# Products of constants on TensorE in four waits between the MLP and the shared units

## The reference

```python
x = x + ln(attention(ln(x), sign-quantised weights))        # 32 heads, 8 key heads, causal
x = x + ln(W2 @ fwht(silu(W1 x) * (W3 x)))                  # MLP, hidden 1024, layer 0
k, v, r = mixes of ln(x) with the row before it, @ Wk, Wv, Wr
x = x + ln((scan over time of k, v) * r @ Wo)               # layer 1, first part
out = sum over the 4 best of 32 experts of c * (silu(x @ wg) * (x @ wu)) @ wd
out = out + sigmoid(x @ seg) * (silu(x @ sg) * (x @ su)) @ sd   # shared expert, 704 wide
x = x + ln(out)
```

## Time and profile before

| | us |
|---|---|
| median of 3 runs | 558.63 |
| lowest and highest | 557.62, 561.06 |
| the profiled execution | 553.65 |
| its span, first to last instruction | 551.8 |
| PE busy | 429.5 (78% of the span) |
| DVE, ACT, POOL busy | 351.8, 271.5, 226.7 |
| mean granted TensorE clock | 0.903 of full |

### The profile page before, as it was taken

The page is one execution under the profiler, slowest core; times in us unless marked ns, Lnnn a source line. Parts: engine busy times, 40 slices in busy tenths (PEclk is TensorE's granted clock), DMA queues, the critical chain, the costliest instruction groups (busy, mean ns, idle before and its releaser), DMA issues.

```text
span 551.8 us, 9885 instructions
## 1 busy us (share of the span) xinstructions
PE 429.5 (78%) x3364; PEld 296.1 (54%) x3364; DVE 351.8 (64%) x857; ACT 271.5 (49%) x519; POOL 226.7 (41%) x301
## 2 busy tenths in 40 slices
PE   2887979998996889696994170687879799999754
PEld 1635435554552378585873160466768466666443
DVE  5558848788871447737468889597663355555336
ACT  8457646766777342233861462332452255556402
POOL 5881424434649402501500452138448045565600
PEclk9979979999999779899999585788989899999958
DMA  7583531111410259100000000699712244454282
GB/s 219 142 135 116 89 58 45 34 40 45 170 37 4 76 172 330 49 1 1 0 2 0 29 29 29 169 210 273 223 51 100 78 123 143 128 143 121 64 310 77
DMA packets 52033, 56.04 MB, mean 102 GB/s; under 512 B 10244, under 2 KB 42893, under 8 KB 51984
## 3 DMA queue, kind: packets, MB, share of 16 engines
q1 hardware_dynamic: 47536, 46.67, 32.0%
q0 software_dynamic: 4448, 8.73, 4.7%
HBM read 35.61 MB, written 21.73 MB: 104 GB/s over the span
## 4 chain that ended last, share of the span: by engine, by line
PE 51%; DVE 22%; issue 7%; ACT 6%; DMA 6%; SPq 4%; POOL 4%; DVEq 0%; ACTq 0%; POOLq 0%
PE ps L2249 7%; PE ps L1982 5%; PE ps L2032 4%; PE ps L1961 4%; PE ps L1940 4%; PE ps L2272 4%; PE ps L2020 4%; PE ps L2230 3%; PE ps L2022 3%; PE ps L2021 3%; DVE st L937 2%; PE ps L1994 2%; DVE h_lo L1104 2%; ACT probs L1625 2%; DMA q_ring<-q_ring 2%
## 5 line engine op out<-in xcount | busy, mean ns | idle before, releaser
L1625 ACT ACTIVATE probs<-ps 128x512 f32<-128x512 f32 x160 | 87.2, 598 | 44.8 <-PE ps L1961 44.0
L1037 DVE TENSOR_REDUCE negm<-ps 128x2 f32<-128x1024 f32 (+1 forms) x64 | 67.6, 1082 | 17.1 <-PE ps L1950 17.0
L845 POOL DMA_INDIRECT y_slots_scratch<-yblk,ids x48 | 47.0, 979 | 49.9 <-issue 29.0
L679 POOL TENSOR_TENSOR rstd<-ve,halfneg 128x4 f32<-128x4 f32 x15 | 16.2, 1078 | 110.3 <-DVE ve L966 46.9
L1982 PE MATMUL ps<-probs,v_all 128*32 128x128 f32 (+3 forms) x512 | 50.6, 475 | 4.9 <-DVE att L1065 3.5
L1940 PE MATMUL ps<-k_all,q_ring 64*128 64x512 f32 (+3 forms) x256 | 46.6, 375 | 8.4 <-DMA q_ring<-q_ring 6.5
L1663 ACT CAST h_hi<-hf 128x512 fp32r<-128x512 f32 x28 | 17.4, 621 | 65.8 <-DVE hf L1095 63.7
L1961 PE MATMUL ps<-q_ring,k_all 64*128 64x512 f32 (+3 forms) x256 | 40.8, 375 | 9.0 <-ACT probs L1625 6.8
L1436 DVE COPY xcol<-ps 128x256 f32<-128x256 f32 x48 | 20.4, 425 | 39.3 <-PE ps L2230 39.3
L1961 PEld LDWEIGHTS ps<-q_ring,k_all 64*128 64x128 f32 x256 | 21.1, 188 | 42.0 <-ACT probs L1625 31.7
L814 POOL DMA_INDIRECT x_sorted_scratch<-rows,dest x32 | 33.0, 1032 | 24.5 <-DVE dest L1353 15.6
(11 more groups left out here) (329 smaller groups left out, 1326.9 us busy)
## 6 DMA issues: line engine op xcount, KB each, us to landing
x_sorted_scratch<-pad SPq DMA_DIRECT2D x6, 1072.0 KB, 12.7
xblk<-x_sorted_scratch SPq DMA_DIRECT2D x96, 67.0 KB
wgu<-in_moe_w SPq DMA_DIRECT2D x4, 1536.0 KB, 17.6
q_ring<-q_parts_scratch SPq DMA_DIRECT2D x64, 64.0 KB
ycomb<-y_slots_scratch SPq DMA_DIRECT2D x8, 512.0 KB, 6.4
wd<-in_moe_w SPq DMA_DIRECT2D x1, 3072.0 KB, 18.8
sraw<-in_moe_w SPq DMA_DIRECT2D x6, 384.0 KB, 3.0
q_parts_scratch<-qparts SPq DMA_DIRECT2D x4, 512.0 KB, 4.9
```

Of the source, the lines that this page charges most:

```text
L845: pool.indirect_dma_start(out=y_slots, out_offset=bass.IndirectOffsetOnAxis(ap=ids[:, i:i + 1], axis=0), in_=yblk[:, i % YR, :], in_offset ...
L1037: dve.tensor_reduce(negm[:, par, :, hp, qt], pair_of, AX.X, ALU.max, negate=True).then_inc(s1_read, 1)
L1625: act.activation(probs[:, par, u, :], ps[:, col_unit(g, u), :], ACT.Exp)\
```

## The change

Four calls of `keep_busy` are added to PE's stream, all with bank 0: 44 products ahead of `transposes(2, 1)`, 20 between them and `keys(1)`, 60 between `values(1)` and `transposes(3, 0)`, 14 between `receptances(1)` and `logits_of(0)`. Each call stands ahead of the wait that follows it.

```diff
             mlp_down(B * HC - 1)
+            keep_busy(44, 0)
             pe.wait_ge(rows_ready, 4 * TPB)
             transposes(2, 1, rows_tile(1))
+            keep_busy(20, 0)
             keys(1)
             mix_out(0)
             values(1)
+            keep_busy(60, 0)
             pe.wait_ge(rows_ready, 5 * TPB)
             transposes(3, 0, rows_tile(0))
             receptances(1)
+            keep_busy(14, 0)
             logits_of(0)
             logit_rows(0)
             shared_up(0)
```

## The result

The changed kernel takes 555.6 us (median of 20 runs), the kernel before 557.84 (20 runs). The ratio is 0.9937, 95% interval [0.9913, 0.9962]: 3.5 us less, between 2.1 and 4.9. It leaves out the slower of two groups into which executions fall, and is not the quotient of the two medians, which lie 2.2 us apart. Forecast were 556.0 us and a gain of 2.6.

A forecast was written before the change was run, and what follows sets the result against it. Short PE bursts alternate with DVE, ACT and POOL row work, slowed by a clock that falls in idle waits. Gains 0.6 + 1.13 + 1.84 = 3.57 us, less 1.0 for one fall, take 2.6 off 558.63: 556.0 us, range 551.5 to 560.0.

The forecast's parts named there:

- Lengths of the fillings: The four PE fillings last 9.8, 4.6, 13.4 and 3.2 us at full clock, each ending within its wait.
- Transposes of turn 2: Eight transposes before the keys run at full clock, 1.09 us instead of 1.97; ACT's copies limit the gain to 0.6 us.
- Keys: Key products at full clock finish before DVE asks, removing its waits of 0.48 and 0.65 us; gain 1.13 us.
- Transposes of turn 3 and receptances: From the transposes to the seventh product, 4.31 us becomes 2.47 at full clock; all counts, gain 1.84 us.
- Routing products gain nothing: Routing products behind the fourth filling already run at full clock, 0.40 us each, so they gain nothing.
- What follows keeps it: Mask, destinations, scatters and first load of sorted rows descend from the logits, so the load comes about 2.6 us sooner.
- The fall of the clock: One fall of PE's clock, in the idleness before turn 2's transposes or in `mix_out`, takes 1.0 us off the gain.
- rival 2: The clock holds throughout the stretch, the full 3.57 us is gained, 555.1 us; chance 0.13.
- Rival 3: Transposes don't speed up in this place, gain only 1.1 us, 557.5 us; chance 0.03.
- Rival 4: Over 1% faster, some 552.6 us, if the runs lose more at half clock here than the trace; chance 0.12.
- Rival 5: Gain swallowed by a later burst falling to half clock, or fillings not holding the clock; 558.6 us, chance 0.14.
- Rival 6: Slower: the two short fillings run wholly at half clock, late by 3.2 and 2.2 us; 564.0 us, chance 0.08.

The follow-up runs named there:

- Experiment 5: The changed kernel with 100 products in place of 60 in the third filling; ratio 1.0052 to the kernel before, 562.37 us.
- experiment 2: The changed kernel without the 44 and the 60, so only the 20 and the 14 stay; ratio 1.0009 to the kernel before.
- experiment 3: The changed kernel with each filling halved to 22, 10, 30 and 7 products; ratio 1.0006 to the kernel before.
- experiment 7: The changed kernel with ten more products inside `mix_out(0)`; ratio 0.99 to the kernel before.
- experiment 8: The changed kernel with fillings lengthened to 52, 24, 67 and 17 and ten more products inside `mix_out(0)`; ratio 0.9916 to the kernel before.
- experiment 10: The changed kernel with only the first site filled (44 and 20), the 60 and 14 removed; ratio 0.9995 to the kernel before.
- experiment 12: The changed kernel with 10 products in `mix_out(0)` and 10 more in the wait for DVE's mask; ratio 0.9861 to the kernel before.
- experiment 4: The changed kernel with each filling product replaced by one f32 transpose of the 128x128 identity, same counts; ratio 0.9999 to the kernel before.
- experiment 11: The kernel before, same code, profiled again for a second trace; 558.75 us against 553.65 for the first profiled execution.
- experiment 1: The changed kernel without the 20 and the 14, so only the 44 and the 60 stay; ratio 0.9983 to the kernel before.
- experiment 9: The changed kernel with only the second site filled (60 and 14), the 44 and 20 removed; ratio 0.9989 to the kernel before.

## Why the prediction was right, step by step

- **Lengths of the fillings**: predicted 9.8, 4.6, 13.4, 3.2; measured 9.67, 4.48, 13.12, 3.20. Right (0.216 us a product, where I took 0.22), and that no filling was late in the changed kernel decided the sign. Experiment 5 shows the price of being late.
- **Transposes of turn 2**: 0.6 predicted, 0.76 measured (keys at 18.84 for 19.60). ACT's two copies now run one behind the other.
- **Keys**: 1.13 predicted, 0.74 measured. DVE's two waits are gone, and `cols_lo` begins 1.32 us sooner behind the keys' start, but it grew by 0.58. In the trace of before it ran behind POOL's work on the shared chunk; now it meets it. DVE and POOL, before:

```profile
323.67 0.68 DVE L1161 TENSOR_TENSOR cols_lo<-den,cols_hi 128x512 fp32r<-128x512 f32 x1
```

```profile
321.24 1.84 POOL L806 TENSOR_TENSOR schunks<-sraw,schunks 128x768 fp32r<-128x768 f32 x1
```

and in the second trace of the changed kernel:

```profile
324.70 1.26 DVE L1161 TENSOR_TENSOR cols_lo<-den,cols_hi 128x512 fp32r<-128x512 f32 x1
```

```profile
323.61 1.81 POOL L806 TENSOR_TENSOR schunks<-sraw,schunks 128x768 fp32r<-128x768 f32 x1
```

  `cols_lo` lasts 1.26 us instead of 0.68, and ends 0.54 us behind POOL's step (325.42). In all nine traces in which it begins during that step (the first and second of the changed kernel, experiments 2, 3, 5, 7, 8, 10 and 12) it takes 1.26 or 1.27; in the five others it begins after it and takes 0.68. The waits that I counted as the gain were time in which POOL had been getting out of the way. The Trainium skill, "VectorE: DVE Perf Modes", section "Two Vector instructions with no wait between them", speaks of a second SBUF read interface that VectorE shares with GpSimd, used by an instruction with two SBUF inputs or in a two-port mode; `cols_lo` has two inputs, and its lengths agree with such sharing. No run here isolates the port. Two inputs are not needed to be held: on the way to the mask another such POOL step begins, and DVE's step beside it is held too. Before, that is a CAST of one input, 1.83 us where the same CAST takes 0.18 at 395.68; in the changed kernel it is the next step, 2.34 us where it takes 0.69 at 361.16 before:

```profile
359.29 1.83 DVE L1253 CAST topf<-topi 128x32 f32<-128x32 uint32 x1
361.16 0.69 DVE L1257 TENSOR_TENSOR eq<-iota,topf 128x512 f32<-128x512 f32 x1
```

```profile
364.72 1.82 POOL L806 TENSOR_TENSOR schunks<-sraw,schunks 128x768 fp32r<-128x768 f32 x1 [9.88 <-ACT schunks L1716]
364.75 2.34 DVE L1257 TENSOR_TENSOR eq<-iota,topf 128x512 f32<-128x512 f32 x1
```

  One of the two is 1.65 us longer in each of the 14 traces, on the way from the logits to the destinations. DVE L1011, ahead of turn 2, meets such a step as well: 1.76 us in every trace, 0.16 at 384.13. These costs are the same before and after the change, and no run here moves the POOL steps.
- **Transposes of turn 3 and receptances**: 1.84 predicted, 2.00 measured (4.58 to 2.58 us). The seventh receptance stands 2.31 us behind the start of the transposes, where I had 2.47.
- **Routing products gain nothing**: wrong by 0.38. I looked at the first products of that burst only; their four small transposes ran at half clock before:

```profile
356.91 0.64 PE L2167 MATMUL ps<-ident,logits_t 34*128 34x34 f32 x4 [0.67 <-ACT logits_t L1694]
```

  and take 0.44 now (362.36 above). Between routing products and DVE's copy 3.07 us became 2.69. This term was missing from the sum. With it the parts are 0.76, 0.74, 2.00 and 0.38.
- **What follows keeps it**: 3.90 at the destinations of batch 0, 3.76 at those of batch 1, 3.4 and 3.7 at the load in the two traces of the changed kernel. Right.
- **The fall of the clock, 1.0 us off**: mis-sized. No fall that costs time happened in either trace of the changed kernel; the one at the mask, which the prediction did not foresee, costs nothing up to the destinations. The full sum, 3.57, forecast as rival 2 with a chance of 0.13, is nearer to what the traces show (3.86), and the ratio's interval (2.1 to 4.9) holds both. That the full sum is only 0.3 off is in part luck: the keys' term was too large by 0.39 and the missing one is 0.38. So is the nearness of 556.0 to 555.6, for the median of the kernel before came out 0.8 us lower in 20 runs than in the 3 that I started from. That falls do happen at these places, with prices near those I gave, the experiments show: within `mix_out` 1.8 and 2.1 us (experiments 2 and 3, 21.98 and 22.31 us for 20.22; up to 2.2 predicted), behind the 60 1.1 and 1.4 us (1 and 9: 3.64 and 3.93 us for 2.58).
- **Rival 3**, transposes that don't speed up, falls by the 1.09 us at both sites of the changed kernel and by experiment 4. The Trainium skill, "TensorE: Matmul & The Clock Gate", Part 4, says that the full clock does not engage in transpose mode; these runs disagree, with 44 transposes in 4.96 us at a granted 1.00.
- **Rival 4**, more than 1% because the runs lose more at half clock here than the trace shows: experiment 11 refutes its ground: that trace is 5.1 us longer than the first, and 4.95 of it lie ahead of the stretch.
- **Rival 5** did not decide the time, but what it feared did happen once: a burst that ran at full clock before, the one behind the mask, falls to half in the changed kernel. It is not on the critical path. Experiments 1 to 3 are what rival 5 looks like where it is: the work is hidden and the gain gone. **Rival 6** did not occur.

**What stays open.** Why the same 2.1 us behind the same 60 products were harmless in four traces (both of the changed kernel, 7, 12) and let the clock fall in two (1 and 9), and the same for the 2.73 us in `mix_out` (harmless in the changed kernel twice, 5 and 10; a fall in 2 and 3). These four falls came where the clock had already been low earlier in the stretch. But that order is no rule. At the mask, behind waits of 2.50 to 2.52 us, the clock fell in eight traces, and in five of them it had been held since the MLP's end (both of the changed kernel, 5, 7, 8); behind 2.49 us in experiment 2, where it had been low, it stayed full. And ahead of the stretch, where the code is the same in all 14 traces, earlier transposes stand behind a wait of 2.96 to 3.00 us. They take 1.09 us in six traces, 1.97 in seven and 1.45 in one, and the kernel before has both: 1.09 at 257.82, and in its second trace

```profile
262.36 1.97 PE L1994 MATMUL ps<-ident,rows 128*128 128x128 f32 x8 [2.97 <-DVE rows L1015]
```

So whether the clock falls in a wait of 2 to 3 us differs between executions of one program, and the falls of experiments 1, 2, 3 and 9 need no other reason. With this I can't say how often a run of the changed kernel loses its gain; only the ratio of its runs averages over that. Nor is it shown that filling more (7 and 8) makes it rarer.

## What to carry to other kernels

Filling a wait on TensorE pays only if the filling reaches the wait's end, for the clock that counts is that of the burst behind it; half of a long filling gave nothing. It must not pass the end, for what lies beyond it is lateness. Fill all the waits of a stretch whose bursts other engines wait for: with one site filled and the other not, the two gains added up to 1.7 us of 3.9, in one trace of each. Even 2 to 3 us left idle can lose the clock in one execution and keep it in the next, so one trace does not settle it. Price the gain not by how much faster the burst gets but by what DVE and ACT really wait for, and look at what the step that now comes earlier meets on the neighbouring engine.

## What the runs showed of the hardware

- Transposes (128 x 128, f32) ran at the granted full clock (44 in 4.96 us), kept it, and were all that PE did while it came back from half to full (experiment 4).
- Behind a wait of 2.96 to 3.00 us in code that is the same in all 14 traces the granted clock was full for eight transposes in six traces, half in seven, and changed within them in one.
- A DVE step that began during a POOL subtraction of 128x768 was held: `cols_lo` lasted 1.26 or 1.27 us instead of 0.68 in nine of nine traces, a CAST with one input 1.83 instead of 0.18, an elementwise step of 128x512 2.34 instead of 0.69. Not every step is: a `decay` from PSUM that began at 322.29 in such a step kept its 0.81 us.
- Two executions of one program differed by 5 us (before) and 6 us (changed) ahead of the stretch, and by less than 0.1 us over the 104 to 107 us behind it.
